# Gated cross-attention with a routed FFN: the values' upper halves read in place, their low halves made on VectorE

## The reference, cut to what matters

```python
x = x + jnp.tanh(g_xattn[0]) * _L0_xattn_ref(_layernorm(x), ctx_1024, ctx_1024, 0, mask)   # keys = values = ctx
x = x + jnp.tanh(g_ffn[0]) * _L0_ffn_ref(_layernorm(x), ...)
# _L0_xattn_ref: x (8, 224, 2048), ctx (8, 750, 512), 32 heads of 64, 8 groups of keys and values
scores = jnp.einsum('bsgrd,btgd->bgrst', xq, xk) / math.sqrt(64) + mask
probs = jax.nn.softmax(scores, axis=-1)
out = jnp.einsum('bgrst,btgd->bsgrd', probs, xv)
```

## Time and profile before

| | us |
|---|---|
| median of three runs | 1170.98 (1170.7 to 1171.06) |
| profiled execution | 1171.02 |
| its span, first to last instruction | 1169.2 |
| PE, DVE, ACT, POOL busy | 1102.4, 947.1, 916.7, 905.7 |

### The profile page before, as it was taken

One profiled execution on the slowest core, in us unless ns is written; L12 is line 12 of the kernel. 1 busy time (PEld: TensorE's weight loads), 2 busy tenths in 40 slices (PEclk: granted clock), 3 DMA queues, 4 the chain that ended last, 5 costly groups with the idle time before them and its releaser, 6 DMA issues.

```text
span 1169.2 us, 40600 instructions
## 1 busy us (share of the span) xinstructions
PE 1102.4 (94%) x17123; PEld 785.9 (67%) x17380; DVE 947.1 (81%) x2261; ACT 916.7 (78%) x1226; POOL 905.7 (77%) x824
## 2 busy tenths in 40 slices
PE   4999999999999999999999999999999999999998
PEld 2677777777777777777777777777777655555554
DVE  5888888888888888888888888888874899676776
ACT  5899998988899899899889998998882443655544
POOL 6899999999999999999999999999992111333424
PEclk9999999999999999999999999999999999999999
DMA  9421231233114212411331132122126600002214
GB/s 343 141 73 49 59 117 42 54 71 106 48 43 105 82 47 56 122 43 44 81 106 48 42 70 55 45 56 60 43 67 196 239 2 1 1 36 109 103 78 180
DMA packets 61620, 95.44 MB, mean 82 GB/s; under 512 B 35329, under 2 KB 44545, under 8 KB 57602
## 3 DMA queue, kind: packets, MB, share of 16 engines
q1 hardware_dynamic: 60722, 91.79, 25.8%
q10 hardware_dynamic: 720, 1.05, 0.2%
HBM read 71.75 MB, written 20.97 MB: 79 GB/s over the span
## 4 chain that ended last, share of the span: by engine, by line
PE 75%; POOL 17%; issue 4%; DVE 2%; DMA 1%; ACT 1%; DVEq 0%; SPq 0%; POOLq 0%
PE psum L964 15%; PE psum L942 13%; PE psum L1010 12%; POOL arena L591 12%; PE psum L951 6%; PE psum L987 6%; PE psum L981 5%; PE psum L982 5%; PE psum L1090 3%; PE psum L997 2%; POOL arena L558 2%; PE psum L920 2%; PE psum L1059 1%; POOL arena L611 1%; POOL arena L599 1%
## 5 line engine op out<-in xcount | busy, mean ns | idle before, releaser
L591 POOL TENSOR_TENSOR arena<-arena 128x768 bf16<-128x768 f32 x448 | 652.7, 1473 | 37.2 <-ACT arena L752 32.8
L1342 DVE CUSTOM_DVE_ANT_0 arena<-psum,arena 128x750 f32<-128x750 f32 x448 | 420.4, 939 | 124.3 <-PE psum L951 112.6
L752 ACT ACTIVATE arena<-psum 128x768 f32<-128x768 f32 x448 | 362.4, 809 | 83.0 <-PE psum L964 81.3
L756 ACT ACTIVATE arena<-arena,neg_max 128x750 f32<-128x750 f32 x448 | 409.7, 914 | 3.7 <-DVE neg_max L1342 3.7
L964 PEld LDWEIGHTS psum<-ident,arena 64*128 64x128 f32 x5376 | 205.3, 138 | 98.4 <-issue 93.0
L964 PE MATMUL psum<-ident,arena 64*128 64x64 f32 x5376 | 263.6, 230 | 6.5 <-ACT arena L752 2.7
L942 PE MATMUL psum<-arena 128*128 128x512 bf16 x674 | 224.1, 387 | 38.6 <-issue 37.8
L981 PEld LDWEIGHTS psum<-arena 128*128 128x128 bf16 (+1 forms) x2688 | 194.4, 98 | 58.1
L982 PE MATMUL psum<-arena 128*128 128x64 bf16 (+1 forms) x2688 | 221.9, 193 | 0.0
L981 PE MATMUL psum<-arena 128*128 128x65 bf16 (+1 forms) x2688 | 221.6, 194 | 0.0
L982 PEld LDWEIGHTS psum<-arena 128*128 128x128 bf16 (+1 forms) x2688 | 178.5, 98 | 53.3
(11 more groups left out here) (170 smaller groups left out, 1200.7 us busy)
## 6 DMA issues: line engine op xcount, KB each, us to landing
arena<-in_k_t SPq DMA_DIRECT2D x128, 187.5 KB, 3.2
arena<-in_v_rows SPq DMA_DIRECT2D x64, 192.0 KB, 2.6
out<-arena SPq DMA_DIRECT2D x10, 1024.0 KB, 3.9
arena<-in_x_top SPq DMA_DIRECT2D x8, 1024.0 KB, 5.6
arena<-in_x_rest SPq DMA_DIRECT2D x8, 768.0 KB, 4.5
spill<-arena SPq DMA_DIRECT2D x96, 64.0 KB, 2.2
arena<-spill SPq DMA_DIRECT2D x6, 1024.0 KB, 10.2
arena<-in_w_t SPq DMA_DIRECT2D x4, 1024.0 KB, 19.8
```

The costliest lines, as they stand in the source:

```text
L591: pool.tensor_tensor(p_lo[:, n % RING, :], p_sb[:, n % RING, :], high(p_sb[:, n % RING, :]), ALU.subtract).then_inc(p_split, 1)
L752: act.activation(p_sb[:, n % RING, :].rearrange("p (c h q) -> p h c q", h=2, q=HALF), turned_ps, ACT.Copy).then_inc(evac_a, 1)
L756: act.activation(s_sb[:, n % RING, 0:CTX], s_sb[:, n % RING, 0:CTX], ACT.Exp, bias=neg_max[:, n % 4, :], scale=-1.0).then_inc(exped, 1)
L1342: dve.tensor_tensor_reduce(s_sb[:, n % RING, 0:CTX], flat_ps[:, score_at(n):score_at(n) + CTX], mask_sb[:, max(n % UNITS - REP + 1, 0), :] ...
```

## The change

- `v_hi` goes, with ScalarE's copy (L765) and its semaphores. `v_raw` gets a 65th float32 column, set to 1.0 once by VectorE; the loads fill columns 0 to 63 of each chunk.
- L981 and L987 read `high(v_raw)` with 65 columns.
- The subtraction moves from GpSimd, m = 2 of the window before, to VectorE, m = 6 of the window before, behind everything else of that step. It subtracts the upper 16 bits and waits for the load itself.
- SP's load of the values for window w+2 moves behind all else of window w, and waits until window w's products with the values are done.

```diff
-        v_raw = carve("attention", [128, 2, NCH, D])
-        v_hi = carve("attention", [128, 2, NCH, D + 1], BF16)
+        v_raw = carve("attention", [128, 2, NCH, D + 1])
...
             def load_v(g):
-                sp.dma_start(v_raw[:, g % 2], v_rows[g].rearrange("p (c d) -> p c d", c=NCH)).then_inc(v_loaded[g % 2], 16)
+                sp.dma_start(v_raw[:, g % 2, :, 0:D], v_rows[g].rearrange("p (c d) -> p c d", c=NCH)).then_inc(v_loaded[g % 2], 16)
...
                 if window + 2 < GROUPS:
-                    sp.wait_ge(v_split, window + 1)
-                    load_v(window + 2)
                     sp.wait_ge(scored, UNITS * (window + 1))
                     load_k(window + 2)
...
                     load_rest(b + 2)
+                if window + 2 < GROUPS:
+                    sp.wait_ge(valued, UNITS * (window + 1))
+                    load_v(window + 2)
...
                 g = window + 1
-                if m == 2 and 0 <= g < GROUPS:
-                    pool.wait_ge(v_hi_done, g + 1)
-                    pool.tensor_tensor(v_lo[:, g % 2], v_raw[:, g % 2], v_hi[:, g % 2, :, 0:D],
-                                       ALU.subtract).then_inc(v_split, 1)
...
-                g = window + 1
-                if m == 0 and 0 <= g < GROUPS:
-                    act.wait_ge(v_loaded[g % 2], 16 * (g // 2 + 1))
-                    if g >= 2:
-                        act.wait_ge(valued, UNITS * (g - 1))
-                    else:
-                        act.wait_ge(v_ones_set, 1)
-                    act.activation(v_hi[:, g % 2, :, 0:D], v_raw[:, g % 2], ACT.Copy).then_inc(v_hi_done, 1)
...
-                    pe.matmul(o, hi, v_hi[0:rows, u, c, :], start=(c == 0), stop=False, skip_group_check=True)
+                    pe.matmul(o, hi, high(v_raw[0:rows, u, c, :]), start=(c == 0), stop=False, skip_group_check=True)
...
-            dve.memset(v_hi[:, :, :, :], 1.0).then_inc(v_ones_set, 1)
+            dve.memset(v_raw[:, :, :, D:D + 1], 1.0)
...
+                g = window + 1
+                if m == 6 and 0 <= g < GROUPS:
+                    dve.wait_ge(v_loaded[g % 2], 16 * (g // 2 + 1))
+                    dve.tensor_tensor(v_lo[:, g % 2], v_raw[:, g % 2, :, 0:D], high(v_raw[:, g % 2, :, 0:D]), ALU.subtract).then_inc(v_split, 1)
```

More of the change, by code:

```diff
@@ L222, in flamingo_block @@
         pads_zero = sem("pads_zero")
-        v_ones_set = sem("v_ones_set")
         gx_loaded = sem("gx_loaded")
@@ L253, in flamingo_block @@
         k_split = sem("k_split")
-        v_hi_done = sem("v_hi_done")
         v_split = sem("v_split")
@@ L986, in value @@
                     lo = p_lo[0:rows, n % RING, c * 128:(c + 1) * 128]
-                    mm = pe.matmul(o, lo, v_hi[0:rows, u, c, :], start=False, stop=(c == NCH - 1), skip_group_check=True)
+                    mm = pe.matmul(o, lo, high(v_raw[0:rows, u, c, :]), start=False, stop=(c == NCH - 1), skip_group_check=True)
                 mm.then_inc(valued, 1)
```

## The result

The changed kernel takes **1174.38 us** (median of 8 runs, the lowest 1173.89) against 1171.11 for the kernel before: ratio **1.0026, 95% interval 1.0017 to 1.0036**, for which one disturbed execution of 2198.54 us is left out. That is 3.0 us slower by the ratio (3.3 by the medians); 1166.9 was forecast. The profiled execution took 1174.2 us with a span of 1172.4, at a granted TensorE clock of 1.0 throughout, as before.

What follows compares the result with a forecast made beforehand. TensorE, busy 94% of the span, was taken to bound the kernel, with ScalarE late in two steps. Terms -4.7 - 0.5 + 0.3 + 0.5 + 0.3 = -4.1 us took 1171.0 to 1166.9 us; range 1164.5 to 1178.

Steps and rivals of the forecast that it cites:

- (e): TensorE's value matmuls read the upper halves in place, every second bf16, as the keys already are: 0.
- first rival: No change, 1171.0 us: ScalarE's 4.7 us given back by TensorE's in-place reads or by busy VectorE; chance 0.13.
- signs of being wrong: New subtractions over 1.2 us, TensorE waiting for them at its first value matmul, or the steps of 1.84 us growing.
- rival 2: Slower: GpSimd goes on first, VectorE's subtraction comes late and TensorE stands; about 1177, up to 1190 us; chance 0.20.
- first long step: TensorE's step 0 to 1, 1.95 instead of 1.84 us, held by ScalarE's normalisation; forecast to stay.
- (a): ScalarE's value copy, 64 x 0.52 us, goes; the second long step (1.92 us) shortens, 52 x 0.09: -4.7 us.
- (b): GpSimd's value subtraction, 64 x 0.89 us, goes; TensorE waits less for GpSimd: -0.5 us, of 0 to -1.7.
- (c): Memset of ones shrinks to 12 columns, at the start beside the first loads: 0.
- (g): SP's queue: the value load moves behind other loads and waits for the values; next key load not reached: 0.
- (d): VectorE subtracts in step 6, 0.55 us each, sometimes contending with GpSimd for SBUF: +0.3 us in all.
- (f): Value loads in 768 packets of 256 B, costing only at the start: +0.5 us, and first subtraction +0.3.
- Rival 3: GpSimd really is the bound where the chain shows it, 14 us gained in windows with w1: 1157 us; chance 0.03.

Runs made afterwards that it cites:

- c1: Kernel before, with ScalarE's copy of the values moved to step 3 and GpSimd's subtraction to step 4, packed values kept: 1169.92 us, 0.9987.
- e1: Kernel before, with only the values' subtraction moved to VectorE in step 6; ScalarE's copy and packed reads stay: 1171.56 us, ratio 1.0005.
- f1: c2 with the subtraction on VectorE in step 6 and packed values: 1164.31 us, ratio 0.9939.
- e2: Changed kernel, with the subtraction on GpSimd in step 4 instead of VectorE; in-place reads and new loads stay: 1175.09 us, ratio 1.0033.
- d1: Changed kernel, with the low-part product also reading in place, 8064 such matmuls instead of 5376 (result wrong): 1180.68 us, ratio 1.0077.
- e3: Changed kernel, with v_raw rows 320 bytes apart instead of 260, all beginning on a multiple of 64: 1172.40 us, ratio 1.0015.
- p1: Changed kernel, with both value buffers starting 32 bytes past a multiple of 64, 260-byte pitch kept: 1171.93 us, ratio 1.0007.
- c2: c1 with ScalarE's normalisations of three windows in eight moved from step 6 to step 2: 1167.76 us, ratio 0.9969.
- m1: Changed kernel plus a prelude timing matmuls per way of reading; total not read; 65 columns: 32.5 to 34.6 ns in place, 30.2 to 31.9 packed.

## Why the prediction was wrong

The step that failed is **(e)**: "TensorE reads the upper halves in place ... 0". It is a term of the sum that was mis-sized; its cost is +9.0 us of value blocks. The outcome is the first rival's mechanism at 1.7 ns a matmul (9.0 us / 5376), carried past the "no change" that its price line stopped at. That line, 5.4 us for each nanosecond, was right; the value put into it was not. Of the signs of being wrong that the prediction names, the one that told was the last: the steps of 1.84 us grew, to 1.87. (The other two showed in three and in two of the 64 windows.) That the measured time lies within the stated range (1164.5 to 1178) is luck: the range reached so far up for the sake of rival 2, which did not occur.

The argument for 0 was that L942's matmuls, in which an in-place and a packed operand alternate, "don't fall into two sorts". They do. In the trace of before the in-place one comes first, takes 0.40 us and starts the packed one 238 ns later; the packed one takes 0.38 and starts the next instruction 217 ns later:

```profile
552.35 0.40 PE L942 MATMUL psum<-arena 128*128 128x512 bf16 x1
552.59 0.38 PE L942 MATMUL psum<-arena 128*128 128x512 bf16 x1
```

So it is in all 226 pairs of which both records are there (237 to 240 ns after the in-place one, but for three; 215 to 218 after the packed one). The summary line of L942 doesn't show it:

```profile
L942 PE MATMUL psum<-arena x674: 377/378/628, 13.8 to 873.2; 128*128 128x512 bf16 x169
```

Half of the in-place records are missing from the trace, so the median, 378, is that of the packed ones. L942's in-place matmul stands behind transposes, which might be a reason of its own; L1010, in the FFN, has none in between. It goes round in threes, in place, packed, in place:

```profile
918.23 0.39 PE L1010 MATMUL psum<-arena 128*128 128x512 bf16 x1
918.46 0.38 PE L1010 MATMUL psum<-arena 128*128 128x512 bf16 x1
918.67 0.39 PE L1010 MATMUL psum<-arena 128*128 128x512 bf16 x1
918.90 0.39 PE L1010 MATMUL psum<-arena 128*128 128x512 bf16 x1
```

By the starts to the nanosecond, over all its unbroken groups of six and twelve, the next matmul follows a packed one after 215 ns and an in-place one after 226. And a short matmul that reads in place was there as well: L1115, 128 columns, goes round in the same threes, 55 ns after a packed one and 58 after an in-place one. That is 11 ns for 512 columns and 3 for 128, some 0.02 ns a column, and so about 1.4 to 1.5 ns for 65 columns; times 5376 that is an estimate of 7.5 to 8.2 us, from the trace of before alone. With it the prediction's sum would have been +3.4 to +4.1 instead of -4.1. The change to in-place reads could have been priced before it was made.

The Trainium skill too speaks for free reads (SBUF — State Buffer, "Door 1: The DMA port swizzle (why `[64,N]` ≈ `[32,N]`)": up to 8 bf16 can be strided for free). For these matmuls the runs disagree, at 65, 128 and 512 columns, by the numbers above and those of the table, and the measurement decides.

Where the rest went. From step lengths over the whole kernel (one unit's first L972 to the next one's, against the same in before), 441 steps together grew by 2.80 us. Step 1 of the table is the first long step, step 2 the second, step 3 the one in which TensorE also turns query rows:

| step of the window | 1 | 2 | 3 | 4 | 5 | 6 | 7 |
|---|---|---|---|---|---|---|---|
| after less before, us over 63 windows | -0.84 | -2.99 | +1.75 | +1.97 | +0.24 | +1.05 | +1.63 |

If all seven carried the slower reads evenly, each would have 9.0 / 7 = +1.3. (Steps 4 and 5 differ because in windows 11 and 19, where GpSimd works on w1 and the normalisation, the one grows by 0.3 us and the other shrinks by 0.4.)

- **(a) ScalarE's copy, -4.7**: right. The second step is 1.3 + 3.0 = 4.3 us better than the reads alone would make it; in c1 it is 1.84 instead of 1.92.
- The first long step, forecast to stay, stays (1.93). But since ScalarE and not TensorE sets its length, the slower reads are hidden in it: 1.3 + 0.84 = 2.1 us that the price of (e) does not show in the time.
- **(b) GpSimd's subtraction, -0.5**: less, some 0.1 us in each of windows 11 and 19. From 100 to 300 us TensorE waits for GpSimd 1.8 us, where it was 1.7:

```profile
PEld psum L972 <- POOL arena L589: 1.0, 2, 0.5
...
PE psum L972 <- POOL arena L589: 0.8, 2, 0.4
```

- **(c) the memset, 0**, and **(g) SP's queue, 0**: TensorE doesn't wait for them. GpSimd waits 2.6 us for key loads instead of 1.8, all of it in the first 39 us, where this differs from run to run anyway.
- **(d) VectorE's subtraction, +0.3**: right in mechanism and price. It got in between two GpSimd instructions, took 0.65 us in the median and held GpSimd's next one up by 0.31 us. TensorE's weight loads waited for it twice, 0.9 us together, both in the first windows, where (f) had put 0.3 for it. What is left of that in the time can't be told from 0: e1 has the same two waits (0.23 and 0.61 us) and gives 0.5 us, with an interval from -0.5 to 1.6. Rival 2 did not occur; three subtractions did take over the 1.2 us that it names, and TensorE waited for none of them.
- **(f) packets of 256 B, +0.8 with the first subtraction**: about 0. There are 40961 packets more (102581 against 61620), and a value load lands after 3.0 us instead of 2.6, but the first unit's L972 comes 0.1 us earlier than before, and the steps of the first three windows grew by 0.4 us, which the slower reads alone would give (7 x (29 + 11 + 29) ns = 0.5). At the start TensorE waits for GpSimd as it did, 0.75 against 0.72 us:

```profile
41.39 0.37 PE L972 MATMUL psum<-arena 128*128 128x65 bf16 x6 [0.75 <-POOL arena L589]
```

The sum as measured: +9.0 (reads) - 4.3 (second step) - 2.1 (first step, hidden) - 0.2 (GpSimd) = +2.4 of the 2.8 us; the 0.4 left over is not settled. The span grew by 3.2: the other 0.4 lies behind the last unit, in a part that the change doesn't touch and whose length differs by up to 0.7 us between the profiled executions (286.5 us before, 287.0 after, 287.2 in f1). **Rival 3** (GpSimd as the bound, 1157) is refuted by e1: GpSimd lost its 17% of the chain, and the time stayed.

Shown by experiments: that the reads and not the shared port make the loss (e1, e2), that it grows with the number of in-place matmuls (d1), that it depends on the addresses (e3, p1), and that the copy's gain is there without them (c1). Not shown: why a step of two and certain row starts cost what they do, and why L942's in-place matmul costs 21 ns where L1010's costs 11. With rows at 0/320, e3's two buffers differ (535, 541) although both begin on multiples of 64, so "start and pitch" is not the whole rule.

## What to carry to other kernels

A pass that is removed from one engine by letting another read in place is paid at every later read: count those reads, and price them on instructions that already read so, one by one. The start of a matmul to the start of the next is the measure; a median over a line that mixes both kinds hid here what single rows show. Where an engine has 94% busy time, a nanosecond or two on 5,000 of its instructions outweighs a whole pass on an engine that has slack; moving the pass to a step where nobody waits got the same gain for nothing (c1, c2, f1). An edit's worth depends on who is late: VectorE's subtraction was worth 0 on the kernel before and 3.5 us once GpSimd's own subtraction stood where it made GpSimd late.

## What the runs showed of the hardware

- The spacing of matmuls depends on how the moving operand lies in SBUF: 29.2 ns for 64 packed columns, 30.2 to 31.9 for 65 packed, 32.5 to 34.6 for 65 read at every second bf16 (m1). At 128 columns it is 55 packed and 58 in place, at 512 it is 215 and 226 (before, L1115 and L1010): 5 to 6% more for every second bf16, at either length. Between two buffers of the same kernel, 24 bytes of offset made 15 ns in 17 matmuls.
- It repeats exactly: the value blocks of e1 and of the kernel before, and those of e2 and of the changed kernel, agree to 0.1 ns in the mean, though other engines' work lay differently. What VectorE and GpSimd did at the same time did not touch TensorE's reads.
- A VectorE instruction that waits for GpSimd gets in between two GpSimd instructions that follow each other without a gap; the later of them takes 1.75 instead of 1.44 us.
- The start varies from run to run: p1's profiled execution waited 3.06 us for its third key load, the changed kernel's 1.88, the kernel before 1.76. That execution of p1 took 1174.39 us, where p1's median is 1171.93. A term of half a microsecond at the start can't be read from one profile:

```profile
39.80 1.44 POOL L558 TENSOR_TENSOR arena<-arena 128x750 bf16<-128x750 f32 x1 [3.06 <-DMA arena<-in_k_t]
```
